# Setup of a fused attention and expert kernel in another order, with transposes of the identity while the loads run

## The reference

```python
Q = LN(x) @ Wq;  K = ctx @ Wk;  V = ctx @ Wv          # to 128 features
out = softmax(Q @ K.T / sqrt(128)) @ V @ Wo + bo + LN(x)
out = out @ Wfc                                        # then a layer norm with gamma, beta
```

## Time and profile before

| | us |
|---|---|
| runs shown (3) | 1028.02, 1028.23, 1026.46 |
| median | 1028.02 |
| profiled execution, whole | 1025.64 |
| its span | 1023.8 |
| TensorE busy in the span | 980.9 |
| VectorE, ScalarE, GpSimd busy | 685.0, 510.7, 404.0 |

### The profile page before, as it was taken

How to read it: one execution, slowest core, us unless ns; L and a number is a source line. 1 busy time by engine, 2 the same in 40 slices (tenths; PEclk the granted TensorE clock), 3 DMA queues, 4 the chain that set the end, 5 groups by cost and what they waited for, 6 DMA issues and landing times. The chain is left out here.

```text
span 1023.8 us, 18460 instructions
## 1 busy us (share of the span) xinstructions
PE 980.9 (96%) x6808; PEld 902.6 (88%) x6808; DVE 685.0 (67%) x1629; ACT 510.7 (50%) x1044; POOL 404.0 (39%) x631
## 2 busy tenths in 40 slices
PE   6999999899999999999999999999999999999995
PEld 5899998588899999987888898899999999999985
DVE  7677777577678888765685555544456677667664
ACT  5446666432477777752445433333335444444442
POOL 5514444507344433415622000000015768767651
PEclk9999999999999999999999999999999999999997
DMA  8200000112688888824215200000001011101000
GB/s 235 83 1 1 1 2 1 40 43 63 196 262 261 257 254 257 263 69 129 67 53 155 42 1 21 2 1 1 1 1 22 20 27 28 32 21 32 17 12 16
DMA packets 56878, 76.51 MB, mean 75 GB/s; under 512 B 5536, under 2 KB 37408, under 8 KB 56800
## 3 DMA queue, kind: packets, MB, share of 16 engines
q1 hardware_dynamic: 40480, 51.61, 16.7%
q0 software_dynamic: 15648, 22.81, 7.7%
q10 hardware_dynamic: 672, 1.05, 0.3%
HBM read 61.43 MB, written 14.02 MB: 74 GB/s over the span
## 5 line engine op out<-in xcount | busy, mean ns | idle before, releaser
L2515 DVE TENSOR_TENSOR XT_lo<-bank,XT_lo 128x512 fp32r<-128x512 f32 x116 | 73.3, 634 | 78.4 <-ACT XT_lo L2175 77.8
L43 PE MATMUL bank<-V_hi,XT_lo 128*128 128x256 f32 x416 | 123.8, 298 | 1.2 <-DVE XT_lo L2515 1.2
L2175 ACT ACTIVATE XT_lo<-bank 128x512 fp32r<-128x512 f32 x116 | 63.8, 552 | 115.5 <-PE bank L1882 114.9
L45 PE MATMUL bank<-V_hi,XT_lo 128*128 128x256 f32 x416 | 117.3, 282 | 0.0
L44 PE MATMUL bank<-V_lo,XT_lo 128*128 128x256 f32 x416 | 117.0, 281 | 0.0
L2520 DVE TENSOR_REDUCE part<-wide 128x1 f32<-128x402 f32 (+1 forms) x116 | 72.4, 624 | 35.4 <-PE wide L45 33.4
L43 PE MATMUL wide<-expert_w_hi,XT_hi 128*128 128x402 f32 (+2 forms) x236 | 93.0, 394 | 1.1 <-DVE XT_hi L2556 0.9
L45 PE MATMUL wide<-expert_w_hi,XT_hi 128*128 128x402 f32 (+2 forms) x236 | 87.1, 369 | 0.0
L44 PE MATMUL wide<-expert_w_lo,XT_hi 128*128 128x402 f32 (+2 forms) x236 | 86.9, 368 | 0.0
L43 PEld LDWEIGHTS bank<-V_hi,XT_lo 128*128 128x128 f32 x416 | 78.4, 189 | 4.6 <-DVE XT_lo L2515 2.9
L44 PEld LDWEIGHTS bank<-V_lo,XT_lo 128*128 128x128 f32 x416 | 79.0, 190 | 0.4
(11 more groups left out here) (499 smaller groups left out, 3272.0 us busy)
## 6 DMA issues: line engine op xcount, KB each, us to landing
sraw<-w1T SPq DMA_DIRECT2D x14, 512.0 KB, 4.8
sraw<-w3T SPq DMA_DIRECT2D x14, 512.0 KB, 4.9
sraw<-w2T SPq DMA_DIRECT2D x14, 512.0 KB, 5.1
raw_even<-w1T SPq DMA_DIRECT2D x11, 512.0 KB, 4.5
raw_even<-w3T SPq DMA_DIRECT2D x11, 512.0 KB, 4.9
raw_even<-w2T SPq DMA_DIRECT2D x11, 512.0 KB, 5.1
XT_hi<-queries POOLq DMA_DIRECT2D x16, 256.0 KB, 3.2
routed_results<-rys POOLq DMA_DIRECT2D x15, 256.0 KB, 4.8
```

The lines of the kernel that those rows point to most:

```text
L43: pe.matmul(out, wh, xh, start=first, stop=False)
L45: return pe.matmul(out, wl, xh, start=False, stop=last)
L2175: act.activation(weights(g, nk, 0), transposed(g, nk), ACT.Copy).then_inc(sem["high"], 1)
L2515: dve.tensor_tensor(weights(g, nk, 1), transposed(g, nk), weights(g, nk, 0).bitcast(F32), ALU.subtract).then_inc(sem["low"], 1)
```

## The change

The setup gets another order on all engines, and nothing is computed otherwise.

- Before its first unit TensorE transposes the identity 28 times into bank 3, as soon as GpSimd has made it.
- Context block 0 goes to ScalarE's queue, in two halves of 256 columns with a semaphore each; tokens 0 go to SyncE's queue, to the place where context 0 was. Context 1 goes ahead of tokens 1; the small bias loads go ahead of context 2; context 2 goes ahead of tokens 2.
- Unit k0 is made in two halves, each after its own half of the low part. High and low parts of context 0 are made by halves.
- The units' order is k0 v0 k1 v1 f k2 v2 q0 q1 q2 q3 v3 k3, with turn 0 after v1, turn 1 after f, turn 2 after q0, turn 3 after q1, and the fold after q2.
- VectorE forms the weights' low part ahead of the statistics, and the low part of context 1 in GpSimd's place. GpSimd forms those of context 2 and of the fold only after VectorE's normalisation of groups 1 and 3, and that of context 3 last.

```diff
-UNITS = [(kind, b) for b in range(3) for kind in "kvq"] + [("f", 0)] + [(kind, 3) for kind in "qkv"]
+UNITS = [("k", 0), ("v", 0), ("k", 1), ("v", 1), ("f", 0), ("k", 2), ("v", 2), ("q", 0), ("q", 1), ("q", 2), ("q", 3),
+         ("v", 3), ("k", 3)]
...
 # context_low(eng, b)
-eng.wait_ge(ctx_high, b + 1)
-eng.tensor_tensor(CT_lo[:, :, x], ctf[:, :, x], CT_hi[:, :, x].bitcast(F32), ALU.subtract)\
-   .then_inc(ctx_low if b else ctx_low0, 1)
+eng.wait_ge(ctx_high, b + 2)
+eng.tensor_tensor(CT_lo[:, :, x], ctf[:, :, x], CT_hi[:, :, x].bitcast(F32), ALU.subtract).then_inc(ctx_low, 1)
+
+def first_half(h):
+    return slice(256 * h, 256 * h + 256)
...
 # sync
 weight("L0_xattn_Wv", lda)
-context(0)
+tokens(0)
 weight("L0_xattn_Wq", ldq)
+context(1)
 tokens(1)
-context(1)
-tokens(2)
 weight("L0_xattn_WoT", ldb)
 weight("L0_xattn_Wfc", ldb)
 weight("L0_ffn_router_wT", ldb)
-context(2)
-tokens(3)
-context(3)
 for t, name in ((BO, "L0_xattn_bo"), (BQC, "L1_xattn_bq_c"), (BKS, "L1_xattn_bk_s"),
                 (BQS, "L1_xattn_bq_s"), (BKC, "L1_xattn_bk_c")):
     sp.dma_start(t, A[name]).then_inc(ldo, 16)
+context(2)
+tokens(2)
+tokens(3)
+context(3)
...
 # scalar
-act.dma_start(X[:, 0:4 * D].rearrange("p (i d) -> p i d", d=D),
-              A["x"][0, 0:512, :].rearrange("(i p) d -> p i d", p=P)).then_inc(ldx[0], 16)
+for h, sem in enumerate((ldc_first, ldc[0])):
+    act.dma_start(ctf[:, :, first_half(h)], A["ctxT"].rearrange("(c p) n -> p c n", p=P)[:, :, first_half(h)])\
+       .then_inc(sem, 16)
...
-context_high(0)
-normalise(0)
+for h, sem in enumerate((ldc_first, ldc[0])):
+    act.wait_ge(sem, 16)
+    act.activation(CT_hi[:, :, first_half(h)], ctf[:, :, first_half(h)], ACT.Copy).then_inc(ctx_high, 1)
 act.wait_ge(ldq, 16)
 act.activation(Wb_hi[:, 0:nq], raw[:, 0:nq], ACT.Copy).then_inc(first_high, 1)
 context_high(1)
 high(0)
-token_high(0)
-normalise(1)
-high(1)
-token_high(1)
-high(2)
-context_high(2)
-normalise(2)
-high(3)
-high(4)
-second_weights()
-token_high(2)
-normalise(3)
-context_high(3)
-high(5)
+high(1)
+second_weights()
+normalise(0)
+context_high(2)
+high(2)
+normalise(1)
+token_high(0)
+high(3)
 act.wait_ge(ldf, 32)
 act.activation(fold_hi[:, :], fold_raw[:, :], ACT.Copy).then_inc(fold_high, 1)
+token_high(1)
+high(4)
+high(5)
+context_high(3)
+normalise(2)
+normalise(3)
+token_high(2)
 high(6)
+high(7)
+high(8)
 token_high(3)
-for u in range(7, 10):
-    high(u)
+high(9)
...
 # gpsimd
 inverse(0)
 inverse(1)
-context_low(pool, 1)
+pool.wait_ge(normal_even, 4)
+context_low(pool, 2)
 inverse(2)
-context_low(pool, 2)
 inverse(3)
-context_low(pool, 3)
+pool.wait_ge(normal_even, 8)
 pool.wait_ge(fold_high, 1)
 pool.tensor_tensor(fold_lo[:, :], fold_raw[:, :], fold_hi[:, :].bitcast(F32), ALU.subtract).then_inc(fold_low, 1)
+context_low(pool, 3)
...
 # vector
+first_weights(0, slice(nq, na))
+for h in range(2):
+    x = first_half(h)
+    dve.wait_ge(ctx_high, h + 1)
+    dve.tensor_tensor(CT_lo[:, :, x], ctf[:, :, x], CT_hi[:, :, x].bitcast(F32), ALU.subtract).then_inc(ctx_low0, 1)
 statistics(0)
-first_weights(0, slice(nq, na))
-context_low(dve, 0)
+first_weights(1, slice(0, nq))
+context_low(dve, 1)
 statistics(1)
+low(0)
 normalise(0)
-first_weights(1, slice(0, nq))
-low(0)
+second_weights()
 normalise(1)
-token_low(0)
+low(1)
 statistics(2)
-low(1)
-token_low(1)
-normalise(2)
 low(2)
 statistics(3)
 low(3)
+token_low(0)
+normalise(2)
+token_low(1)
 low(4)
 normalise(3)
 token_low(2)
-second_weights()
 low(5)
 low(6)
+low(7)
 token_low(3)
-for u in range(7, 13):
+for u in range(8, 13):
     low(u)
...
 # tensor, in unit(u), kind "k"
+if b == 0:
+    for h in range(2):
+        pe.wait_ge(ctx_low0, h + 1)
+        x = first_half(h)
+        for c in range(DC):
+            m = mm3(pe, bank[:, x], kh[:, c, :], kl[:, c, :], CT_hi[:, c, x], CT_lo[:, c, x],
+                    h == 0 and c == 0, h == 1 and c == DC - 1)
...
+pe.wait_ge(ident_known, 1)
+for _ in range(28):
+    pe.transpose(banks[3][:, 0:P], ident[:, :], ident[:, :])
 pe.wait_ge(first_low, 1)
-unit(0)
-pe.wait_ge(ident_known, 1)
+for u in range(4):
+    unit(u)
 turn(0)
-unit(1)
+unit(4)
 turn(1)
-pe.wait_ge(first_low, 2)
-unit(2)
-unit(3)
-unit(4)
-turn(2)
 unit(5)
 unit(6)
+pe.wait_ge(first_low, 2)
+unit(7)
+turn(2)
+unit(8)
 turn(3)
-for u in range(7, 10):
-    unit(u)
+unit(9)
 fold()
```

More of the change, by code:

```diff
@@ L2858, in build @@
                 ldc = sems(ctx, "ldc0 ldc1 ldc2 ldc3")
+                (ldc_first,) = sems(ctx, "ldc_first")
                 (first_high, first_low, second_high, second_low, ctx_high, ctx_low0, ctx_low, fold_high, fold_low, folded, fold_kept,
@@ L3140, in unit @@
                         elif kind == "k":
-                            if b:
-                                pe.wait_ge(ctx_low, b)
[L3143 to L3148, removed]
+                            if b == 0:
[5 more added lines that the diff above has]
+                                                h == 0 and c == 0, h == 1 and c == DC - 1)
+                            else:
+                                pe.wait_ge(ctx_low, b)
+                                x = ctx_cols(b)
+                                for c in range(DC):
+                                    m = mm3(pe, bank[:, 0:x.stop - x.start], kh[:, c, :], kl[:, c, :], CT_hi[:, c, x], CT_lo[:, c, x],
+                                            c == 0, c == DC - 1)
                         elif kind == "v":
                             tiles = ctx_tiles(b)
+                            if b == 3:
+                                pe.wait_ge(ctx_low, b)
                             for t in tiles:
@@ L3194, in _ @@
                         unit(u)
-                    pe.wait_ge(unit_low, 7)
+                    pe.wait_ge(unit_low, 8)
                     x = slice(2 * 512, 3 * 512)
```

## The result

The changed kernel took 1022.05 us in the median of 8 runs (1021.46 to 1025.13), the kernel before 1026.69 (8 runs, 1025.46 to 1028.23): ratio 0.9955, 95% interval 0.9943 to 0.9968, so 4.6 us faster (3.3 to 5.9). Forecast were 4.1 us less than a median of 1028.02, which further runs moved to 1026.69; 1022.05 lies 0.35 us under the range given. The same kernel measured in two further series, each beside the kernel before, gave 0.9964 (0.9952 to 0.9977) and 0.9952 (0.9939 to 0.9966), 3.3 and 3.9 us between the medians. The three together say about 4 us: 3.9 by the medians, 4.4 by the ratios.

What follows compares the result with a forecast made beforehand. TensorE's time and the time before it starts were taken as the bound; its setup terms summed to 35.4 us against 39.60, 4.1 us taken off the 1028.02 median, forecasting 1023.9 us, range 1022.4 to 1026.6.

Steps and rivals of the forecast that it cites:

- The gain: Whole kernel: the setup ends 4.2 us earlier, taken as 4.1 us off the kernel's time; chance of the forecast 0.55.
- That TensorE's time in the setup is the kernel's time: Setup: a microsecond won there is won at the end, since the attention has 58.85 us of work in 59.17.
- The level: Starting time: profiled execution of 1025.64 us, 2.4 us under the median of 1028.02, giving 1021.5 profiled and 1023.9 forecast.
- The sum: Setup on TensorE: 7.65 + 26.6 + 0.04 + 0.8 + 0.3 = 35.4 us for the last unit's end, before 39.60.
- 0.8, at q(2): Setup, unit q(2): TensorE wants its input at 27.65 us, low(5) is ready at 28.4, so it waits 0.8 us.
- the five small loads ... no cost: SyncE's queue: they cost 2.5 us of issuing; context 2 lands about 14.1 us, wanted at 15.2, so no cost.
- Rival A: Start of setup: transposes don't raise the clock; gain only 2.0 to 2.5 us, 1025.5 to 1026.0 us; chance 0.23.
- 0.9 us of v(0) passes at half speed: Term of Rival A in unit v(0): 0.45 us lost, with 1.15 in k(0) making 1.6 us.
- the clock comes up 3.5 us after TensorE's start: Start of setup: clock up after 3.5 us, as before, so the 28 transposes end at 6.3 us.
- Rival B: Setup loads: context 1 at 10.25 us, or weights or halves 1 us later; gain 3.1, 1024.9 us; chance 0.14.
- C: After the setup: a later phase waits for something else and the gain stops there; 1028 us; chance 0.05.
- D: ScalarE held by the fold's loads, delaying turn(2): slower, 1031 us if they land at 27 us; chance 0.03.

Runs made afterwards that it cites:

- the early start alone: Transposes, context 0 in halves on ScalarE's queue, tokens 0 on SyncE's, weights' low part first, old order otherwise, in the kernel before: attention at 45.21 us (before 40.87).

## Why the prediction was right and wrong

**The gain.** 4.1 us were forecast, 4.6, 3.3 and 3.9 measured between medians; the trace shows 3.1 to 3.4. So the nearness of 4.1 to the measured times is luck in part: in the trace, for which it was worked out, the sum was 1 us too good. That TensorE's time in the setup is the kernel's time held: what follows it is no longer but for the clock. The rest between times and traces, 0.5 to 0.8 us by the medians and up to 1.3 by the ratios, isn't explained by any profile. The mean granted clock doesn't explain it either: it was the same on both sides in the two further series (0.992 and 0.993, without one run that reads 0.943), though a late first rise doesn't show in it, since the record reads 1.00 up to there.

**The level**, which put the time outside the range, failed at the step "it lies 2.4 us under the median of 1028.02, from which I forecast". Three runs of a kernel whose runs spread over 3 us don't fix its median to better than 1.3 us, and that error was not in the range: its low end allowed half a microsecond of scatter. The term was 1.33 us too high (1028.02 for 1026.69 in 8 runs); from 1026.69 the same 4.1 us give 1022.6, 0.5 us from what was measured. The spread is in good part the clock's: falls at 250 and 480 us come in some runs and not in others. Of the changed kernel's 8 runs, the four with a mean granted clock of 0.995 took 1021.46 to 1022.15 us, the three at 0.992 or less 1024.14 to 1025.13. The row at 1014.13 had shown such a fall behind idle time; I had not looked for others in the middle.

**The sum** put the end of the last unit at 35.4 us; it came at 36.49. The start was better than worked out (6.93 for 7.65, the weights having landed 0.8 us earlier). The work was right to 0.2 us. The waits were not: forecast 0.8, at q(2); found 0.65 at k(1), 0.55 at turn(0), 0.25 at k(2), 0.9 at q(2), start to start, 2.4 in all. So q(2)'s was right in place, cause and size. K(1) began at 11.72, and 11.75 had been forecast: its input was late by only 0.17 us (11.67 for 11.5), but TensorE, 0.7 us ahead, now had to wait for it. So the better start was given back whole at k(1), and by itself it moved nothing. Turn(0) failed at "the five small loads ... no cost": I followed what lies behind them and not the one who waits for them, ScalarE, for whom they ended at 13.4, where the working has it go on at 12.6; turn(0) began at 16.40 and not at 15.8.

**Rival A**, that transposes don't raise the clock, fell: k(0) ran 0.12 us a matmul in 10 of the 11 profiles that began with transposes, the eleventh being the one with 2.30 us of idle time behind them. The rule in the Trainium skill's page "TensorE: Matmul & The Clock Gate", section "Part 4: PE-mode transpose", is not what this chip showed. But its price was mis-sized by far, in the step "0.9 us of v(0) passes at half speed": without the transposes the loss was 7.4 us in one profile, nothing in another, and 2 to 4 us between medians. The working took for granted that the clock comes up 3.5 us after TensorE's start; in that one profile 19 us of busy time, 10 of them products of the v units, didn't bring it up, and in the other it came after 3.3.

**Rival B** didn't come: context 1 landed at 9.35 and not at 10.25, and k(1) started at 11.72 and not at 12.7. **C and D** didn't either: the fold's loads were in by 19.95 when ScalarE came.

## What to carry to other kernels

A forecast of half a per cent needs the spread of the kernel before, not the median of three runs: look through the whole trace for stretches at the low clock first, and compare kernels at a mark in the trace (here the next phase's first matmul) that such falls don't move. An engine that comes earlier to a wait has won nothing: follow the start through to the first input that it has to wait for. When loads are put ahead of others, ask who waits for them as well as who stands behind. And a warm-up is only worth what the order behind it keeps: here the transposes in the old order brought nothing, the early start with them lost by the clock what it had won, and the new order without them had no gain that could be told.

## What the runs showed of the hardware

- TensorE stayed at the low clock while it was busy without a gap: 19 us of k, v, turn and f, 0.21 us a matmul of 128 or 256 columns, in one execution; in another execution of the same program it rose after 3.3 us. In the kernel with the early start alone it was low for 10.2 us (turn, v, turn, q).
- Back-to-back transposes of fp32 raised it 3.0 to 6.1 us after the first, in all 11 profiles that began with them.
- It fell in or right behind idle times of 1.75 to 4.0 us (2.30 and 4.0 in the setup, 1.75 to 3.31 near 480 to 490 us, 2.92 at the end). But it stayed up behind idle times of 2.12, 2.40 and 2.42 us near 480 to 490 us in three other executions, and always behind 0.4 to 1.67 us; so the length of the idle time alone doesn't decide.
- It also fell, in 12 of 16 profiles, with no idle time at all, at a row of products of 40 columns 3.4 us long, for 3.4 us or twice that, and didn't in the two where the row was cut in two.
- VectorE's normalisation from SBUF took 2.70 us for a pair beside a GpSimd operation and 0.73 without it. Its statistics took 1.40 us for a group either way (in the changed kernel at 17.71 beside one, at 7.56 without).
